# Neighbourhood attention and a ternary feed-forward block on one core: one step less lag, values ahead of scores, square tiles added on GpSimd

## The reference, cut to what matters

```python
# attention: 16 heads of 64, blocks of 16 tokens, window = 5 blocks back and
# forward plus the first token; later tokens are masked
sim  = einsum('bhnid,bhnjd->bhnij', qw, kw)
attn = stable_softmax(where(mask, -max, sim))
attn = einsum('gh,bhnij->bgnij', w_th, attn)        # heads are mixed
out  = einsum('bhnij,bhnjd->bhnid', attn, vw)
x    = layernorm(x + out @ w_out + b_out)
# feed-forward, 128 -> 512 -> 128, both weights made ternary
def ternary_linear(x, w):
    rms = sqrt(sum(x * x)) / sqrt(d)
    return einsum('bsd,fd->bsf', x / (rms + EPS), w_q)
h = gelu(ternary_linear(x, w_up))
x = layernorm(x + ternary_linear(h, w_down))
```

## Time and profile before

| | us |
|---|---|
| three timed runs | 242.18, 241.5, 242.18 (median 242.18) |
| profiled execution, its own time | 243.09 |
| its span, first to last instruction | 241.3 |
| busy: TensorE matmuls | 226.1 (94%) |
| busy: VectorE, ScalarE, GpSimd | 176.6, 164.1, 92.6 |
| mean of one reciprocal of the row sums, one `rows_low` | 0.20, 2.40 |

### The profile page before, as it was taken

How to read it: one execution, slowest core, us unless ns; L and a number is a source line. 1 busy time by engine, 2 the same in 40 slices (tenths; PEclk the granted TensorE clock), 3 DMA queues, 4 the chain that set the end, 5 groups by cost and what they waited for, 6 DMA issues and landing times.

```text
span 241.3 us, 10011 instructions
## 1 busy us (share of the span) xinstructions
PE 226.1 (94%) x4343; PEld 203.1 (84%) x4343; DVE 176.6 (73%) x461; ACT 164.1 (68%) x311; POOL 92.6 (38%) x111
## 2 busy tenths in 40 slices
PE   7999899999999999999999999999999989989970
PEld 7899789888999999888988998888988977889750
DVE  0674699987777882688766885688468999785864
ACT  2686466776666648985599559964898334988652
POOL 7035204531343342444515454536254353120542
PEclk9999999999999999999999999999999999999975
DMA  6937560020020001100200111010201001000002
GB/s 217 293 101 209 165 139 7 7 61 3 3 58 13 24 3 39 35 21 8 65 3 4 48 34 36 3 46 4 68 3 29 20 3 46 1 4 22 3 3 87
DMA packets 19107, 11.69 MB, mean 48 GB/s; under 512 B 2232, under 2 KB 18168, under 8 KB 18936
## 3 DMA queue, kind: packets, MB, share of 16 engines
q1 hardware_dynamic: 18324, 10.47, 15.3%
q10 hardware_dynamic: 740, 0.59, 0.8%
HBM read 8.91 MB, written 2.10 MB: 46 GB/s over the span
## 4 chain that ended last, share of the span: by engine, by line
PE 57%; DVE 15%; ACT 8%; issue 7%; POOL 6%; SPq 2%; DMA 2%; POOLq 0%; DVEq 0%; ACTq 0%
PE bank L1108 9%; PE bank L1110 8%; PE bank L1109 8%; PE bank L1257 7%; PE bank L1231 6%; PE bank L1215 4%; DVE CTl L876 4%; POOL gTl L533 2%; DVE AT L881 2%; POOL xw L506 2%; DMA raw<-in_L_attn_x 2%; SPq L395 2%; DVE sm L896 2%; PE bank L1327 2%; PE bank L1189 2%
## 5 line engine op out<-in xcount | busy, mean ns | idle before, releaser
L577 ACT ACTIVATE Yb<-bank 128x512 f32<-128x512 f32 x64 | 38.4, 601 | 28.4 <-PE bank L1110 27.9
L519 POOL TENSOR_TENSOR E<-E,rc 128x400 f32<-128x400 f32 x32 | 27.9, 871 | 77.3 <-DVE rc L898 77.3
L876 DVE TENSOR_TENSOR CTl<-bank,CTh 128x512 fp32r<-128x512 f32 x64 | 41.1, 683 | 22.3 <-ACT CTh L577 22.1
L1108 PE MATMUL bank<-xTh,Gh 128*128 128x256 f32 x128 | 39.4, 308 | 1.7 <-ACT Yb L577 1.5
L1108 PE MATMUL bank<-CTh,Mh 128*128 128x256 f32 x128 | 37.0, 289 | 0.6 <-DVE CTl L876 0.6
L577 ACT ACTIVATE CTh<-bank 128x512 fp32r<-128x512 f32 x64 | 34.8, 600 | 2.5 <-PE bank L1257 2.4
L1110 PE MATMUL bank<-CTh,Ml 128*128 128x256 f32 x128 | 36.1, 282 | 0.0
L724 ACT ACTIVATE E<-E 128x400 f32<-128x400 f32 x32 | 17.3, 541 | 27.5 <-DVE E L890 27.4
L1109 PE MATMUL bank<-CTl,Mh 128*128 128x256 f32 x128 | 36.0, 281 | 0.0
L1109 PE MATMUL bank<-xTl,Gh 128*128 128x256 f32 x128 | 35.8, 280 | 0.0
L1110 PE MATMUL bank<-xTh,Gl 128*128 128x256 f32 x128 | 35.7, 279 | 0.0
(11 more groups left out here) (142 smaller groups left out, 469.3 us busy)
## 6 DMA issues: line engine op xcount, KB each, us to landing
raw<-in_L_attn_x SPq DMA_DIRECT2D x37, 64.0 KB
pt_rows<-PT SPq DMA_DIRECT2D x2, 512.0 KB, 4.7
R<-pt_rows SPq DMA_DIRECT2D x1, 1024.0 KB, 5.6
xr<-in_L_attn_x SPq DMA_DIRECT2D x6, 128.0 KB
out<-y SPq DMA_DIRECT2D x6, 128.0 KB, 1.9
raw<-in_L_attn_x SPq DMA_DIRECT2D x13, 56.0 KB
w_sb<-in_L_attn_w_qkv SPq DMA_DIRECT2D x2, 256.0 KB, 4.7
w_sb<-in_L_attn_w_qkv ACTq DMA_DIRECT2D x2, 256.0 KB, 4.5
```

What stands on the lines that cost most here:

```text
L519: tt(e, e, rc[s % 2][:, :].unsqueeze(2).broadcast_to([P, TILES, WIN]), ALU.mult).then_inc(s_norm, 1)
L577: copy = lambda o, i, **k: nc.scalar.activation(o, i, ACT.Copy, **k)
L876: v.tensor_tensor(ct_view(CTl[s // 4 % 2], s % 4, q), c_view(s, q), ct_view(f32(CTh[s // 4 % 2][:, :, :]), s % 4, q), ALU.subtract).then_i ...
L1108: mm(o, wh, rh, start=start, stop=False, **k)
```

## The change

- TensorE's order from step 8 on is `c_part(s-2)`, `scores(s)`, `transposes(s-1)`, and the rest as before; step 7 (TURN) does both the old and the new set. ScalarE and VectorE follow with `ct`, then `at`; on VectorE `at_lo`, `input_scale` and `up_input` stand behind `shift`.
- The lag of `o_part` is 6 steps and chunks start their feed-forward at steps 10, 14, 18, 22, 26 and 30, so chunk 4 has k up to 5 in the loop.
- On ScalarE `gelu` stands right behind the exponential and ahead of `y_out(s, 1)`.
- In chunks 0 to 4 GpSimd adds hidden tiles 2 and 3 of the squares to tiles 0 and 1 (`fold_squares`, behind `hidden_low` and ahead of `normalise`), and `square_sum` reads two tiles. It is called inside `scores`, ahead of the mask matmul.
- The lists behind the loop lose chunk 4's steps and are reordered; some banks change; `keep_busy` is called with 4, 4 and 14 in place of 5.

The diff, with blank and most context lines cut and eight columns of indentation taken off:

```diff
@@ -56,7 +56,8 @@
...
 LAG = 2
-O_LAG = 7
+O_LAG = 6
+TURN = 7
 NT = B * N // P
...
@@ -202,6 +203,7 @@
...
     "f_rstd2", "f_out"))
+f_folded = sem("f_folded")
 f_ss, f_shift2, f_out7 = map(sem, ("f_square_sum", "f_shift2", "f_out_last"))
...
@@ -279,19 +281,20 @@
...
-    if s < 28:
-        return [divmod(s - O_LAG, 4)] if s >= O_LAG else []
-    return {28: [(5, 1), (5, 2)], 29: [(5, 3)], 30: [(6, 0)], 31: []}[s]
-FIRST = [11 + 4 * n for n in range(5)] + [30]
+    if s < TURN:
+        return []
+    early = {7: [(0, 0), (0, 1)], 31: [(6, 1), (6, 2)]}
+    return early.get(s, [divmod(s - O_LAG, 4)])
+FIRST = [10 + 4 * n for n in range(6)]
...
-    return [(n, s - first) for n, first in enumerate(FIRST) if -1 <= s - first < (9, 9, 9, 9, 5, 1)[n]]
-UP_BANK = {5: (0, 2), 6: (0, 2), 7: (6, 5)}
+    return [(n, s - first) for n, first in enumerate(FIRST) if -1 <= s - first < (9, 9, 9, 9, 6, 1)[n]]
+UP_BANK = {5: (1, 0), 6: (2, 0), 7: (6, 5)}
 AT_BANK = {7: 5}
-XT_BANK = {5: 4, 7: 5}
+XT_BANK = {5: 2, 7: 5}
 DN_BANK = {5: 4, 6: 3, 7: 0}
...
@@ -309,14 +312,11 @@
...
-def c_bank(s, q):
-    return bank[(0, 2)[q] if s == 30 else C_BANK[q]]
 def y_bank(s, b):
...
 def squared(n):
-    return gT[0] if n < 4 else gT[2] if n % 2 else gsq
+    return gT[0] if n < 5 else gT[2] if n % 2 else gsq
...
@@ -343,7 +343,7 @@
...
 def c_view(s, q):
-    return c_bank(s, q)[:, :].rearrange("p (r h s) -> p r h s", r=2, s=BLK)
+    return bank[C_BANK[q]][:, :].rearrange("p (r h s) -> p r h s", r=2, s=BLK)
...
@@ -532,6 +532,11 @@
...
+    def fold_squares(n):
+        pool.wait_ge(f_sum, 2 * n + 2)
+        tt(gT[0][:, 0:2, :], gT[0][:, 0:2, :], gT[0][:, 2:4, :], ALU.add).then_inc(f_folded, 1)
     def hidden_root(n):
...
@@ -545,9 +550,10 @@
...
         for n, k in ffn(s):
-            if k == 4 and n < 4:
+            if k == 4:
                 hidden_low(n, 0)
                 hidden_low(n, 1)
+                fold_squares(n)
             if k == 5:
...
@@ -556,16 +562,17 @@
...
                 last_root(n)
-        if s % 4 == 1 and s < STEPS - 4:
-            rows_high((s + 3) // 4)
+        if s == 1:
+            rows_high(1)
+        if s % 4 == 2 and 2 < s < STEPS - 4:
+            rows_high((s + 2) // 4)
         if s % 4 == 0 and s > 0:
...
+    last_root(4)
     variance_roots(6)
     variance_roots(7)
-    hidden_root(4)
     hidden_root(5)
-    last_root(4)
     hidden_root(6)
...
@@ -679,11 +686,11 @@
...
         o = slice(2 * t, 2 * t + 2)
-        if n < 4:
+        if n < 5:
             act.wait_ge(f_gl, 2 * n + t + 1)
...
             act.wait_ge(f_gl, 12)
-        elif n > 5:
+        elif n > 6:
             act.wait_ge(f_ss, n - 1)
...
@@ -705,24 +712,33 @@
...
             act.wait_ge(s_small, 32)
-        if s > LAG:
+        if LAG < s <= TURN:
             ct_hi(s - LAG - 1)
-        if 0 < s < O_LAG:
+        if 0 < s < TURN:
             y_out(s, 0)
-        if s >= LAG:
+        if LAG <= s <= TURN:
             at_hi(s - LAG)
-        if s == 0 or s >= O_LAG:
+        if s == 0 or s == TURN:
             y_out(s, 0)
-        if s < O_LAG:
+        if s >= TURN:
+            ct_hi(s - 2)
+            at_hi(s - 1)
+        if s > TURN:
+            y_out(s, 0)
+        if s < TURN:
             y_out(s, 1)
         for n, k in ffn(s):
-            if k == 4 and n < 4:
+            if k == 4:
                 squares(n, 0)
...
         nc.scalar.activation(e, e, ACT.Exp).then_inc(s_exp, 1)
-        if s >= O_LAG:
+        for n, k in ffn(s):
+            if k == 2:
+                gelu(n, 0)
+                gelu(n, 1)
+        if s >= TURN:
             y_out(s, 1)
...
@@ -730,46 +746,34 @@
...
         for n, k in ffn(s):
-            if k == 4 and n < 4:
+            if k == 4:
                 down_out(n)
...
                 x1_hi(n)
-            if k == 3 and n < 4:
+            if k == 3:
                 hidden_high(n, 0)
                 hidden_high(n, 1)
-            if k == 2 and n < 4:
-                gelu(n, 0)
-                gelu(n, 1)
-            if k == 8 and n < 3:
+            if k == 8:
                 result(n)
-    at_hi(30)
-    ct_hi(29)
-    gelu(4, 0)
+    ct_hi(30)
     at_hi(31)
-    ct_hi(30)
-    gelu(4, 1)
-    ct_hi(31)
     x1_hi(5)
     stage(6)
-    hidden_high(4, 0)
-    hidden_high(4, 1)
-    squares(4, 0)
-    squares(4, 1)
+    ct_hi(31)
     gelu(5, 0)
...
     hidden_high(5, 1)
-    result(3)
     x1_hi(6)
+    result(4)
     squares(5, 0)
     stage(7)
+    squares(5, 1)
     gelu(6, 0)
...
     hidden_high(6, 1)
-    down_out(4)
-    squares(5, 1)
     down_out(5)
...
@@ -782,7 +786,6 @@
...
     down_out(7)
-    result(4)
     result(5)
...
@@ -1005,41 +1008,36 @@
...
             dve.wait_ge(s_pt, 32)
-        if s > LAG:
+        if LAG < s <= TURN:
             ct_lo(s - LAG - 1)
-        if s >= LAG:
+        if LAG <= s <= TURN:
             at_lo(s - LAG)
+        if s > TURN:
+            ct_lo(s - 2)
+        shift(s)
+        if s == TURN:
+            ct_lo(s - 2)
         for n, k in ffn(s):
-            if k == 5 and n == 3:
+            if k == 5:
+                dve.wait_ge(f_back, n + 1)
                 hidden_sum(n)
+        if s >= TURN:
+            at_lo(s - 1)
         for n, k in ffn(s):
...
                 up_input(n)
-        shift(s)
-        for n, k in ffn(s):
-            if k == 5 and n < 3:
-                hidden_sum(n)
-            if k == 5 and n == 3:
-                second_sum(n)
-            if k == 6 and n == 3:
-                second_norm(n)
-            if k == 0 and n == 5:
-                residual(n)
-        if s == STEPS - 1:
-            input_scale(5)
-            up_input(5)
         if s < 2:
...
             ternary(0)
-        if 4 <= s < O_LAG:
+        if 4 <= s < TURN:
             fills(IN_STEP[s - 1][-1:])
...
         for n, k in ffn(s):
-            if k == 5 and n < 3:
+            if k == 5 and n < 4:
                 second_sum(n)
...
@@ -1055,45 +1053,42 @@
...
         for n, k in ffn(s):
-            if k == 0 and n < 5:
+            if k == 0:
                 residual(n)
-            if k == 6 and n < 3:
+            if k == 6:
                 second_norm(n)
-    at_lo(30)
-    ct_lo(29)
+    input_scale(5)
+    up_input(5)
+    ct_lo(30)
     at_lo(31)
-    ct_lo(30)
+    x1_lo(5)
+    second_sum(4)
     ct_lo(31)
-    x1_lo(5)
+    second_norm(4)
     residual(6)
-    hidden_low(4, 0)
-    hidden_low(4, 1)
+    result_shift(4)
+    hidden_low(5, 0)
     input_scale(6)
     up_input(6)
-    hidden_low(5, 0)
     hidden_low(5, 1)
...
     hidden_low(6, 1)
+    hidden_sum(5)
     input_scale(7)
-    hidden_sum(4)
     up_input(7)
-    second_sum(4)
+    second_sum(5)
     x1_lo(7)
-    hidden_sum(5)
-    second_norm(4)
-    second_sum(5)
+    second_norm(5)
     hidden_sum(6)
     hidden_low(7, 0)
-    second_norm(5)
     hidden_low(7, 1)
-    result_shift(4)
     second_sum(6)
+    result_shift(5)
     hidden_sum(7)
     second_norm(6)
-    result_shift(5)
     second_sum(7)
...
@@ -1216,7 +1211,7 @@
...
-    def scores(s):
+    def scores(s, sums=()):
...
@@ -1230,6 +1225,9 @@
...
                    start=(tile == 0), stop=False, skip_group_check=True)
+        for n in sums:
+            pe.wait_ge(f_dS, n + 1)
+            square_sum(n)
         if s % (2 * SLOTS) == 0:
...
@@ -1242,10 +1240,7 @@
...
         pe.wait_ge(s_ATl, s + 1)
-        need(pe, s_CTl, 60 if s == 31 else 2 * s if s < 30 else 0)
-        if s == 30:
-            pe.wait_ge(s_sub, STEPS)
-            pe.wait_ge(s_Ye, 64)
+        need(pe, s_CTl, 2 * s)
         if s % 4 == 0:
...
@@ -1254,7 +1249,7 @@
...
                     row = slice(64 * q, 64 * q + WIN)
-                    ins.append(mm(c_bank(s, q)[:, col], xw[s // 4 % 2][row, m, c, :], AT[row, a, col],
+                    ins.append(mm(bank[C_BANK[q]][:, col], xw[s // 4 % 2][row, m, c, :], AT[row, a, col],
                                   start=(n == 0), stop=(n == 2)))
...
@@ -1272,10 +1267,8 @@
...
         pe.wait_ge(f_stage, n + 1)
-        if n < 5:
+        if n < 6:
             need(pe, f_gelu, 2 * n)
-        elif n == 6:
-            pe.wait_ge(f_gelu, 10)
         for i in range(CT):
...
@@ -1288,12 +1281,10 @@
...
-        if n < 5 and t == 0:
+        if n < 6 and t == 0:
             need(pe, f_y2, CT * n)
-        if n == 4 and t == 1:
-            pe.wait_ge(f_res, 6)
-        if n == 6:
-            pe.wait_ge(f_gelu, 11 + t)
+        if n == 6 and t == 1:
+            pe.wait_ge(f_gelu, 12)
         pe.wait_ge(f_xTl, n + 1)
...
@@ -1319,14 +1310,18 @@
...
-        pe.wait_ge(f_sum, 2 * n + 2)
+        if n < 5:
+            pe.wait_ge(f_folded, n + 1)
+        else:
+            pe.wait_ge(f_sum, 2 * n + 2)
         need(pe, f_hss, n)
+        tiles = 2 if n < 5 else FT
         for i in range(CT):
-            for t in range(FT):
+            for t in range(tiles):
                 for lo in range(0, P, 32):
...
```

(50 more changed lines are left out.)

## The result

| | before | after |
|---|---|---|
| median of 5 runs on one chip, us | 241.83 (241.46 to 242.18) | 239.65 (239.33 to 240.08) |
| ratio, 95% interval | | 0.991 [0.9891, 0.9929] |
| profiled execution: its own time, span | 243.09, 241.3 | 239.48, 237.7 |
| mean granted clock | 0.98 | 0.98 |

The changed kernel is faster by 2.2 us in the medians, by 3.6 us in the two profiled executions (243.09 is above each of the five timed runs of before, so the 3.6 flatters the change). 239.3 was forecast.

What follows compares the result with a forecast made beforehand. TensorE was taken as the bound, busy 226.1 of 241.3 us. Terms summed to -0.9 ahead of `attn_back(7)` and -2.0 behind it, together -2.9, set against 242.18 to 243.09: 239.3 us, range 235.6 to 243.2.

Steps and rivals of the forecast that it cites:

- Yb wait: TensorE's second query product waits 0.52 us for ScalarE's `Yb` copy; forecast to go, four times, 2.1 us.
- gTl wait: Second half of `down` waits 0.24 us for `gTl` on GpSimd; forecast to go, four times, 1.0 us.
- (1): Square sums of chunks 0 to 3, halved and placed inside `scores`: 4 x 0.42 = 1.7 us less, GpSimd's add just hidden.
- (2): GELU behind the exponential, first query copy ahead of it on ScalarE: the 0.52 wait for `Yb` goes four times, 2.1 us.
- rival of the table switch: Table switches hold ScalarE 1.28 us longer than their record, ten times, giving 252.1 us; chance 0.01.
- (3): Values ahead of scores, transposes behind them: new loop waits +1.8 us, the wait for `gTl` gone, -1.0.
- Three places: New waits in a round: 0.15 behind the GELU, 0.25 at the `down` step's transposes, 0.4 at `x1_T`.
- (4): One step less lag, ahead of `attn_back(7)`: +1.4 us work, -2.0 old waits, +2.7 new waits taken from 3.4 counted.
- given back in the last steps: VectorE stays the bound between steps 28 and 31, loop gains become waits, the clock falls as before: 242.0 us; chance 0.14.
- (5): Behind `attn_back(7)`: `down`'s second half about 1.2 us earlier, 0.8 from 17 more `keep_busy` matmuls holding the clock; 2.0 taken.
- Slower: Transposes wait for the normalised tile in every step; at 0.25 us a step, 244.6 us; chance 0.15.
- The waits hardly show: VectorE and ScalarE keep pace, new loop waits near 0 and tail waits near 1: 235.8 us; chance 0.20.

Runs made afterwards that it cites:

- e1: Changed kernel without the add on GpSimd, square sums of chunks 0 to 4 over four tiles again: 240.25 us, ratio 0.9924 to the kernel before.
- e2: Changed kernel with GELU back behind the second query copy, at the end of the step: 244.07 us, ratio 1.0069 to the kernel before.
- e3: Changed kernel with the transposes ahead of the scores instead of behind them: 248.04 us, ratio 1.0258 to the kernel before.
- e4: Changed kernel with 14 matmuls whose result is not read at the end of step 29: 238.54 us, ratio 0.9852 to the kernel before.
- e6: Changed kernel with `keep_busy` as before, 5 matmuls behind `up(7)` and none elsewhere: 239.11 us, ratio 0.988 to the kernel before.
- e7: Kernel before, with only the GpSimd add of square tiles and two-tile sums in chunks 0 to 3: 241.5 us, ratio 0.997 to the kernel before.
- e5: Changed kernel with `input_scale` and `up_input` ahead of AT's low part on VectorE: 238.45 us, ratio 0.9851 to the kernel before.
- e9: Changed kernel itself, unedited, timed again: 239.85 us, ratio 0.9887 to the kernel before.

## Why the prediction was right, and which of its steps were not

The time, 239.3 for 239.65, is right, and so are the sign and most of the places. The sum came out since errors in both directions cancelled, and that is luck: by the profiles the new waits cost more than forecast, and two gains that were not counted, or counted too low, paid for them. On the spans the loop lost 3.7 us where 3.0 were forecast, what stands between it and `attn_back(7)` grew by 1.8 for 2.1 (the 1.6 ahead of step 8 taken in), and the end lost 1.7 for 2.0.

In the round, by the distances of starts in the two profiles: the Yb wait -0.62 and the gTl wait -0.35, each with the slow restart behind it (0.22 or 0.23 instead of 0.12 to the second matmul); the sums -0.44; new waits +1.16, with the restart behind `x1_T` and the values product; the transposes -0.75. That is -1.0, as measured (25.97 to 24.96).

(1) *Fewer square sums, -1.7: absorbed.* The size was right: with the restart behind them the sums took 0.84 us before (160.61 to 161.68, less two spacings) and take 0.40 now (151.66 to 152.91, less the 0.85 of a step without them). 0.29 of it is the halving (e1), the rest the place inside `scores`. The failed step is another: the gain was booked in full beside a wait at `x1_T` in the same step. What ends that step is x1n on VectorE, and the step is as long as before (6.65 for 6.64). By e1 the add is worth nothing in the rounds and 0.54 at two other places. That GpSimd just hides it held.

(2) *GELU behind the exponential, -2.1: right.* The Yb wait is gone and what is late next is what was named; e2 gives the 2.2 back, and 2.3 with it that weren't counted, since in the new order AT has less slack. The rival of the table switch is out. The GELU starts 1.30 us after its load starts, and the load 0.02 us after the exponential ahead of it ends (137.63). The Trainium skill ("ScalarE: Activation LUTs", What ACT_TABLE_LOAD costs) gives a drain of about 1380 ns on top of the load. The trace disagrees: between load and activation it has 0.02 us, at both switches of the round.

(3) *The order, waits of +1.8, -1.0 for gTl: the places right, the size low, and a gain missed.* Three places were named and all three wait: 0.22, 0.25 and 0.39 of idle time, for 0.15, 0.25 and 0.4; by the starts 0.3, 0.27 and 0.54. I had found 0.8 a round and taken 0.4, without a row that spoke for the half; 0.86 stands there, and 1.1 in the measure of the forecast. What pays for it is what I didn't see: the transposes cost 0.1 to 0.3 less a step in their new place (e3). The step took the cost of an operation as its own, when it hangs on what follows. The row of before shows it with one neighbour only.

(4) *The lag: the sum near, the shape wrong.* TensorE idles for 3.2 us between step 28 and `attn_back(7)` (36.88 less 33.67), where 3.4 were counted and 2.7 taken. Three of the named places show: `o_part(7, 0)` 0.51, `x1_T(6)` 0.27, `c_part(31)` 0.37; `up(5)` hardly waits. But 1.8 spread over four steps came as one wait of 1.99, at the values product of step 29. I had asked of step 29 only how long its chain is, not that a table load and two GELUs stand ahead of CTh on ScalarE when `queries` is gone from TensorE and covers nothing. The rival "given back in the last steps" has loop gains turn into waits there, and in that it was right in part; but the clock fall that it names is the old one at the end. The fall in step 30, 1.5 us more (e4), stands in none of the forecasts. A reading was off too: the wait of 0.64 for CTl lies in the first of the two stretches of the last steps, not in the second.

(5) *The end, -2.0: -1.7, one of its two causes wrong.* By the order of the lists the second half of `down(7)` starts 0.8 us sooner (10.2 us behind `attn_back(7)`, before 11.1), where 1.2 were forecast; without the 17 matmuls it is 1.4 (9.7 in e6). The full clock gives the other 0.9: 0.5 in that half (1.15 to 0.67 us up to the sums) and 0.4 behind it (7.96 to 7.56). It is not the doing of `keep_busy`: e6 has it without. Shorter waits in the lists are what is left as its cause; that was not tried by itself. And the -1.7 compares one execution with one: e7, whose end is that of the kernel before, takes 19.6 us there and not 20.2.

*Rivals.* "Slower" names a real mechanism: with 0.9 us less slack e3 pays 8.4 us. It didn't come since the slack holds in plain steps. "The waits hardly show" fell with 0.86 a round. (Its time is 235.8; the range was set with 235.6.)

*Open:* of six traces with a wait of 1.98 to 2.02 us ahead of step 30 five have the fall; e5's, with the longest wait, has not, and one of the six runs of e9 has a higher mean clock. What else decides isn't told by these runs.

## What to carry to other kernels

A saving on the bounding engine counts only up to the next operand in the same step: look for the wait behind it, and shorten that queue first (here the order of four lines on VectorE was worth 1.2 us, and the add on GpSimd next to nothing). Where work leaves the last steps, look again at what it covered, above all a table load ahead of a copy that another engine's order hangs on. Fill a long wait with matmuls only where the profile shows the clock falling behind it: 14 in one place gave 1.1 us, 17 in another cost some 0.5 by the traces.

## What the runs showed of the hardware that was not expected

- Four 128x128 transposes behind a values product cost 0.58 to 0.59 us of TensorE's time ahead of 128x32 score matmuls and 0.41 ahead of 128x256 products; behind the mask matmul and ahead of such products, 0.36. No wait stands in any of them.
- After 1.98 to 1.99 us idle the granted clock fell from 1.00 to 0.50 while the engine was fully busy again, in each of five traces: the step behind the wait took 6.45 to 6.49 us at a mean clock of 0.74, and 4.95 to 4.96 at 1.00 where the wait was filled. In one more execution, after 2.02 us idle in the same place, the clock stayed at 1.00.
- At half busy (0.98 of 2.00 us) the clock was 1.00 between 226 and 228 us in e6.
- A GELU table load of 1.28 us began 0.02 us behind the instruction ahead of it and ended 0.02 us before the next one began (137.63 to 138.95).
